# A chain of small transformer blocks on one core: transposes of the next tokens first, another vector order, values projected later, the feed-forward bias as a weight row

## The reference

```
x = x + attn_a(layernorm(x))         # latent attention, 16 heads
x = x + ffn4(layernorm(x))           # fp4-quantised gated feed-forward
x = x + forget_attention(layernorm(x))
x = x + ffn4(layernorm(x))
x = x + conv(layernorm(x))
x = x + local(layernorm(x))          # two layers, below
x = x + linear_attention(layernorm(x))
x = x + local(layernorm(x))          # the same two layers again
```

```
h = shift_token(x)                       # the second 64 columns come from the token before
q, k, v = split(h @ wqkv)                # 8 heads of 64
q, k = rotary(l2norm(q)*qs, l2norm(k)*ks)
x = x + softmax(q k^T in a window of 64, causal) v @ wo
h = layernorm(shift_token(x)) * lg + lb
a, g = split(h @ w1 + b1)                # 341 columns each
x = x + (a * gelu(g)) @ w2 + b2
```

## Time and profile before

| what | us |
|---|---|
| median of the runs shown | 2193.34 |
| the profiled execution's own time | 2203.51 |
| its span, first to last instruction | 2201.7 |
| PE busy | 1819.8 (83%) |
| DVE busy | 1407.5 (64%) |
| ACT busy | 942.4 (43%) |
| POOL busy | 454.2 (21%) |

### The profile page before, as it was taken

One profiled execution on the slowest core, in us unless ns is written; L12 is line 12 of the kernel. 1 busy time (PEld: TensorE's weight loads), 2 busy tenths in 40 slices (PEclk: granted clock), 3 DMA queues, 4 the chain that ended last, 5 costly groups with the idle time before them and its releaser, 6 DMA issues.

```text
span 2201.7 us, 34222 instructions
## 1 busy us (share of the span) xinstructions
PE 1819.8 (83%) x10946; PEld 1445.6 (66%) x11003; DVE 1407.5 (64%) x3623; ACT 942.4 (43%) x2559; POOL 454.2 (21%) x350
## 2 busy tenths in 40 slices
PE   7999966654566888898888799999968988888887
PEld 6888854222355777676676677777847766776676
DVE  4655689556896666676757445655547767566673
ACT  3444422110213555546454363353225464555544
POOL 2200010000013333332424100000014324233340
PEclk9999977555778999999999899999879999999998
DMA  3000000000100000000000000000000000000000
GB/s 133 0 0 0 1 0 0 1 0 0 48 0 1 3 1 2 3 2 4 1 2 1 3 1 0 0 0 0 0 1 4 2 2 1 4 2 3 2 1 22
DMA packets 15104, 13.89 MB, mean 6 GB/s; under 512 B 11286, under 2 KB 14138, under 8 KB 14650
## 3 DMA queue, kind: packets, MB, share of 16 engines
q1 hardware_dynamic: 15034, 13.01, 1.8%
HBM read 9.87 MB, written 1.05 MB: 5 GB/s over the span
## 4 chain that ended last, share of the span: by engine, by line
PE 45%; issue 30%; DVE 16%; ACT 7%; POOL 1%; DVEq 1%; POOLq 0%; ACTq 0%
PE bank L1558 5%; PE bank L1526 4%; PE bank L1546 4%; PE bank L1695 3%; PE bank L1642 3%; PE bank L1537 3%; DVE arena_attn L916 3%; PE bank L1655 2%; PE bank L1677 2%; DVE arena_ffn L901 2%; PE bank L1720 2%; PE bank L1699 2%; DVE probT L686 2%; ACT L1264 2%; PE bank L1743 2%
## 5 line engine op out<-in xcount | busy, mean ns | idle before, releaser
L534 POOL TENSOR_TENSOR arena_ffn<-arena_ffn 128x1024 f32<-128x1024 f32 x60 | 141.5, 2359 | 561.7 <-DVE arena_ffn L901 561.7
L686 DVE COPY probT<-bank 128x512 f32<-128x512 f32 x288 | 197.1, 684 | 70.7 <-PE bank L1537 70.4
L518 POOL TENSOR_TENSOR rstd<-var,mhalf 128x2 f32<-128x2 f32 x48 | 33.4, 696 | 902.6 <-DVE var L641 902.6
L1546 PE MATMUL bank<-vF,probT 128*128 128x64 f32 x1536 | 203.0, 276 | 1.7
L1546 PEld LDWEIGHTS bank<-vF,probT 128*128 128x128 f32 x1536 | 191.3, 196 | 12.9 <-DVE probT L686 12.2
L530 POOL TENSOR_TENSOR inv<-ssq,mhalf 128x16 f32<-128x16 f32 x64 | 188.2, 2940 | 33.6 <-DVE ssq L910 29.9
L1526 PE MATMUL bank<-arena_setup 128*128 128x192 f32 (+1 forms) x1024 | 171.6, 300 | 7.2 <-ACT arena_setup L1317 5.6
L679 DVE TENSOR_REDUCE nmaxF<-bank 128x2 f32<-128x384 f32 (+1 forms) x192 | 114.7, 597 | 88.9 <-PE bank L1526 88.9
L1368 ACT ACTIVATE arena_conv<-bank,nmaxF 128x192 f32<-128x192 f32 x256 | 105.6, 420 | 147.9 <-DVE nmaxF L679 95.1
L1526 PEld LDWEIGHTS bank<-arena_setup 128*128 128x128 f32 x1024 | 154.3, 191 | 11.8 <-issue 0.4
L897 DVE TENSOR_TENSOR arena_ffn<-bank,rope 128x512 f32<-128x512 f32 x128 | 87.7, 685 | 115.0 <-ACT arena_attn L1308 115.0
(11 more groups left out here) (258 smaller groups left out, 4302.4 us busy)
## 6 DMA issues: line engine op xcount, KB each, us to landing
packF<-in_packF SPq DMA_DIRECT2D x1, 3250.0 KB
arena_history<-in_packG SPq DMA_DIRECT2D x1, 2560.0 KB, 9.0
HS<-XH SPq DMA_DIRECT2D x32, 63.5 KB
X<-in_x_tiled SPq DMA_DIRECT2D x1, 1024.0 KB, 4.8
out_dram<-X SPq DMA_DIRECT2D x8, 128.0 KB, 1.9
arena_setup<-in_const_masks_a SPq DMA_DIRECT2D x1, 512.0 KB, 5.4
arena_setup<-in_const_masks_f SPq DMA_DIRECT2D x1, 512.0 KB
HS<-XH SPq DMA_DIRECT2D x32, 0.2 KB
```

The costliest lines, as they stand in the source:

```text
L534: pool.tensor_tensor(t1[:, t], t1[:, t], t2[:, t], ALU.add).then_inc(sems["rope_sum"], 1)
L686: dve.tensor_copy(probT[:, u % 2], bank[4 + u % 2][:]).then_inc(sems["pt_copied"], 1)
L1546: ins = pe.matmul(o, probT[:, u % 2, n * P:(n + 1) * P], val, start=first, stop=(kt == keys // P - 1), skip_group_check=True)
```

## The change

On PE the token transposes of the next batch come first in the step, behind a wait for the copies of v that was further down; the projections of both halves of v move to slot 8, behind the transposes of the output of half 0. On ACT the priming of the gelu table is taken out of `gelus`, and `shifted` comes between it and the gelus. On DVE `gated` moves ahead of the copy and rotary part of its slot, and `hidden_stats` behind the rotary part of slot 5. The bias b2 becomes row 341 of w2, that is row 113 of its third chunk; row 113 of the third chunk of ff is set to one by a fill on POOL once in each `local`, and `hidden_out` runs three matmuls of 114 rows for each half instead of four.

```diff
--- before.py
+++ after.py
@@ -69,7 +69,7 @@
 F_LAYOUT = []
 for _l in range(2):
     F_LAYOUT += [(f"wqkv{_l}", 3 * FH * FHD), (f"wo{_l}", 4 * C), (f"w1_{_l}", 2 * HID), (f"w2_{_l}", 3 * C),
-                 (f"ln_g{_l}", 1), (f"ln_b{_l}", 1), (f"b1_{_l}", 6), (f"b2_{_l}", C)]
+                 (f"ln_g{_l}", 1), (f"ln_b{_l}", 1), (f"b1_{_l}", 6)]
 G_LAYOUT = [("wqkvG", 3 * LH * LHD), ("wgG", LH * LHD), ("woG", 8 * C)]
 
 
@@ -372,7 +372,7 @@
         def zeros_by(n):
 
 
-            return N_POOL_FILL + sum((plan[m] == "conv") + (plan[m] == "win" and plan[m - 1] != "mlp")
+            return N_POOL_FILL + sum((plan[m] == "conv") + 2 * (plan[m] == "win" and plan[m - 1] != "mlp")
                             for m in range(n + 1))
 
         def opens(n):
@@ -592,6 +592,8 @@
                 if kind == "win":
 
                     pool.wait_ge(sems["xh_ready"], v.before("xh_ready"))
+                    pool.memset(ff[96:P, NCH - 1], 1.0).then_inc(setup_pool, 1)
+                    pool.wait_ge(setup_pool, zeros_by(n) - 1)
                     pool.memset(probW[:], 0.0).then_inc(setup_pool, 1)
                     if not opens(n - 1):
                         stage_copy(0)
@@ -947,12 +949,12 @@
                     if s < F_UNITS:
                         t, heads, keys = attn_unit(s, 2)
                         attn_max(v, i, s, len(heads), keys - F_FROM[t], nmaxF, F_SCORE_BANKS)
+                    if m and s == 1:
+                        gated(*m)
                     if s >= 2:
                         attn_copy(v, i, s - 2)
                     if m and s == 4:
                         mlp_end(m[0], m[1])
-                    if hid and s == 5:
-                        hidden_stats(*hid)
                     if nxt:
                         if s in (1, 4):
                             rope_part(vn, ni, nl, s // 4, 0)
@@ -962,8 +964,8 @@
                             norms(vn, ni, s // 6, sch)
                         if s == 7:
                             scaled(vn, ni, 0)
-                    if m and s == 1:
-                        gated(*m)
+                    if hid and s == 5:
+                        hidden_stats(*hid)
                     if hid and s == 7:
                         hidden_apply(*hid)
                     if s == 6:
@@ -1339,7 +1341,6 @@
 
             def gelus(v, i, l):
 
-                prime(ACT.Gelu)
                 for c in range(NCH):
                     n = FROWS[c]
                     src = (bank[7][0:n, 0:T], bank[7][0:n, T:2 * T], bank[6][0:n, T:2 * T])[c]
@@ -1355,10 +1356,12 @@
                 if nxt:
                     vn, ni, _ = nxt
                 if m:
+                    prime(ACT.Gelu)
+                if nxt:
+                    shifted(vn, ni)
+                if m:
                     gelus(*m)
                     prime(ACT.Exp, 1)
-                if nxt:
-                    shifted(vn, ni)
                 for u in range(F_UNITS):
                     t, heads, keys = attn_unit(u, 2)
                     act.wait_ge(sems["max_ready"], v.at("max_ready", i, u + 1))
@@ -1587,10 +1591,12 @@
                 v, nxt, m, hid = around(n, l, i)
                 if nxt:
                     vn, ni, nl = nxt
+                pe.wait_ge(sems["v_ready"], v.at("v_ready", i, NT))
+                if nxt:
+                    transpose_x(vn, ni, bank[2])
                 if m:
                     hidden_gates(*m, 0)
                 pe.wait_ge(sems["qkT_ready"], v.at("qkT_ready", i, NT))
-                pe.wait_ge(sems["v_ready"], v.at("v_ready", i, NT))
 
                 def scores(h, t, keys):
                     return qTF[:, h // 2, t * P:(t + 1) * P], keysZ[:, h // 2, h % 2, F_FROM[t]:keys]
@@ -1606,8 +1612,6 @@
 
                 def between(s):
 
-                    if nxt and s == 0:
-                        transpose_x(vn, ni, bank[2])
                     if m and s == 0:
                         pe.wait_ge(sems["down_used"], v.at("down_used", i, 0))
                         hidden_gates(*m, 1)
@@ -1615,10 +1619,11 @@
                         project_qk(vn, ni, nl, s // 4)
                     if m and s == 1:
                         hidden_values(*m)
-                    if nxt and s in (7, 8):
-                        project_values(vn, ni, nl, s - 7)
                     if s == 8:
                         transpose_y(0)
+                        if nxt:
+                            for t in range(NT):
+                                project_values(vn, ni, nl, t)
                     if m and s == 3:
                         hidden_out(*m)
                     if s == 3:
@@ -1671,11 +1676,9 @@
             def hidden_out(v, i, l):
                 pe.wait_ge(sems["f_ready"], v.at("f_ready", i, NCH))
                 for t in range(NT):
-                    pe.matmul(bank[7][:, t * P:(t + 1) * P], ones1[:], f_at[f"b2_{l}"][0:1, :], start=True, stop=False)
                     for c in range(NCH):
-                        n = FROWS[c]
-                        ins = pe.matmul(bank[7][:, t * P:(t + 1) * P], ff[0:n, c, t * P:(t + 1) * P],
-                                        f_at[f"w2_{l}"][0:n, c * C:(c + 1) * C], start=False, stop=(c == NCH - 1))
+                        ins = pe.matmul(bank[7][:, t * P:(t + 1) * P], ff[0:FCH, c, t * P:(t + 1) * P],
+                                        f_at[f"w2_{l}"][0:FCH, c * C:(c + 1) * C], start=(c == 0), stop=(c == NCH - 1))
                 ins.then_inc(sems["m_down_ready"], 1)
 
             def hidden_alone(v, i, l):
@@ -2032,8 +2035,8 @@
     for l in range(2):
         b1 = a["L1_ffn_b1"][l]
         f.update({f"wqkv{l}": a["L1_ffn_wqkv"][l], f"wo{l}": chunk_rows(a["L1_ffn_wo"][l], P), f"w1_{l}": a["L1_ffn_w1"][l],
-                  f"w2_{l}": chunk_rows(a["L1_ffn_w2"][l], FCH), f"ln_g{l}": a["L1_ffn_ln_g"][l][:, None],
-                  f"ln_b{l}": a["L1_ffn_ln_b"][l][:, None], f"b2_{l}": a["L1_ffn_b2"][l][None],
+                  f"w2_{l}": chunk_rows(np.concatenate([a["L1_ffn_w2"][l], a["L1_ffn_b2"][l][None]]), FCH), f"ln_g{l}": a["L1_ffn_ln_g"][l][:, None],
+                  f"ln_b{l}": a["L1_ffn_ln_b"][l][:, None],
                   f"b1_{l}": np.concatenate([chunk_rows(b1[:HID, None], FCH), chunk_rows(b1[HID:, None], FCH)], 1)})
     w["packF"] = pack(F_LAYOUT, f)
     w["packG"] = pack(G_LAYOUT, {"wqkvG": a["L1_attn_b_w_qkv"], "wgG": a["L1_attn_b_w_gate"], "woG": chunk_rows(a["L1_attn_b_w_out"], P)})
```

## The result

The changed kernel took 2237.51 us (median of 4 runs, 2236.01 to 2239.29), the kernel before beside it 2194.28 (4 runs, 2189.93 to 2195.74): ratio 1.0201, 95% interval 1.0183 to 1.0218. The forecast was 2184, range 2158 to 2206. The profiled execution took 2237.54; its span is 33.7 longer than before.

The account below looks back on a forecast made before the run. It took an ACT, PE, DVE chain in each step as the bound. Plain steps at -0.37 and the other steps and tails summed to -9.8 us: 2193.7 profiled, 2184 as median, range 2158 to 2206.

Parts of the forecast that it names:

- rival (c): PE waits ahead of the output transposes make the clock fall once a step, about +23 us, 2206; chance 0.14.
- finishing steps of the first `local`: Five steps that also finish a batch; forecast to come to 34.95 plus clock falls in three, -5.4 us together.
- tokens first: Next tokens' copies before the gelus on ACT: exponentials of unit 1 come 1.0 us earlier per plain step.
- bias row: Two bias matmul pairs leave PE's chain ahead of unit 1's transposes: 0.82 us a step, 1.15 with gate product first.
- gate product first: `gated` ahead of the rotary on DVE: the wait of 0.17 for it goes, 0.3 us from start to start.
- statistics behind the rotary: Hidden statistics later on DVE: POOL's sum starts later and clamp L910 ends 0.68 us later per plain step.
- values later, and the last ACT wait: Value projections between output transposes and unit 5's product, +1.6 us; ACT's wait for the last q and k closes, -0.5.
- the head: First part of a plain step: tokens first, bias row and gate product first bring unit 2's copy 2.15 us earlier.
- Rival (b): Clamp L910 issues ahead of POOL's sum, saving about 1.2 us in each of 28 steps: 2150; chance 0.15.
- (a): Wait for the last q and k stays, so plain and finishing steps gain nothing: 2193; chance 0.20.
- (d): Token copies find their transposes late, so the 1.0 us is lost in 26 steps: 2210; chance 0.06.
- The second steps: Second step of each `local`, with a hidden norm but no feed-forward: +1.8 us each, to near 30.2.

Follow-up runs that it names:

- experiment 14: Changed kernel with values and statistics as before, plus eight unused 128x128 PE transposes in slot 7: 2117.82 us, ratio 0.9616 to the kernel before.
- 13: Changed kernel with values and statistics as before, plus one unused 128x512 matmul in slot 7: 2117.74 us, ratio 0.9618 to the kernel before.
- 16: Changed kernel plus one unused 128x512 matmul ahead of each of PE's two waits (slots 7 and 8): 2179.93 us, ratio 0.9909 to the kernel before.
- kernel 2: Changed kernel with the values projected in their old place, slots 7 and 8: 2158.44 us, ratio 0.9827 to the kernel before.
- kernel 4: Kernel before with only the values moved to slot 8, behind the output transposes: 2267.75 us, ratio 1.0319 to the kernel before.
- 15: Kernel before with only the values moved, plus one unused 128x512 matmul ahead of each of PE's two waits: 2216.17 us, ratio 1.0067.
- 11: Changed kernel with values in their old place and hidden statistics ahead of the rotary as before: 2121.22 us, ratio 0.9665 to the kernel before.
- 10: Kernel before with only the next tokens transposed and copied first: 2165.17 us, ratio 0.9871 to the kernel before.
- 8: Kernel before with only the feed-forward bias as a weight row: 2167.29 us, ratio 0.9871 to the kernel before.
- kernel 3: Changed kernel with both values in slot 8 but ahead of the output transposes: 2145.3 us, ratio 0.9769 to the kernel before.
- experiment 9: Kernel before with only the values moved, plus both value projections made once more, unused, ahead of the wait for the attention output: 2263.49 us, ratio 1.0322.
- 5: Kernel 3 with POOL's rotary sum of half 1 ahead of the hidden deviation: 2173.9 us, ratio 0.9907 to the kernel before.
- 6: Changed kernel with POOL's rotary sum of half 1 ahead of the hidden deviation: 2230.47 us, ratio 1.0154 to the kernel before.
- kernel 7: Changed kernel with the hidden statistics ahead of the rotary part of slot 5 again: 2190.67 us, ratio 0.9994 to the kernel before.

## Why the prediction was wrong

**The step that failed is the dismissal of rival (c): the sum has nothing for a fall of the clock.** The prediction named the fall, and then said that by the rule on transposes "this rival becomes unlikely, 2184 stands; by idle time alone it is likely", and "the trace leans to the rule". It gave it 0.14. The rule in the Trainium skill (TensorE: Matmul & The Clock Gate, Part 4: PE-mode transpose), that transposes do not count as work for the clock gate, does not hold as it was used: eight transposes in a wait kept the granted clock at 1.00 in the plain steps of experiment 14, as a matmul did in 13. In the plain steps of the changed kernel the clock does not fall between the last value product and the output projection, where the prediction looked. It falls in PE's waits for the copied probabilities and for the output, and fillers in those waits stop it (16). These waits were forecast at 1.4 and 2.4 and are 1.45 and 2.16, or 1.30 for the second where the clock has already fallen and the product between them takes 1.97 in place of 1.10.

The prediction leaned on the finishing steps of the first `local`, and there its place is right: the clock falls at their end, behind waits of 1.28 and 0.72 among transposes. Before, the output projection (L1642) takes 2.84 at 1175.49 in place of 1.95, in kernel 13 it takes 3.21 at 1108.55, in spite of the filler further up. Where a plain step of kernel 2 has a fall, it comes in that stretch as well (granted clock 0.53 and 0.62 from 848 to 852), behind a wait of 1.25. No run filled those waits, so whether transposes count for less there stays open.

**Its size was off too.** The prediction priced a fall at 0.9 to 1.0, from steps before, where it hits the values of half 0 and the work behind them (granted clock 0.64 from 951 to 955 us) and costs 0.89. Here it hits the output transposes and both projections, which the change had just put in a row on the chain. From the start of the output transposes to those of q and k it is 4.71 in the short step shown, 5.81 in the long one and 3.05 in kernel 16: 1.66 and 2.76 more, and these are the differences of the whole steps (35.29 and 36.39 against 33.63). In the mean of the plain steps it is 35.86 - 33.63 = 2.2 each, in kernel 4 1.7. Over all stretches: 2237.51 against 2179.93, 58 us, or 1.8 a step of 32. Rival (c) reached 2206 and should have reached some 2240. It also counted one fall in five steps before, where 9 of the 26 plain and finishing steps have 0.95.

**The terms, at a clock of 1.00.** A cost of the fillers would be in the figures of 13, 15 and 16; 11, and the 1.69 of 15 above, show none.

| term of a plain step | predicted | measured |
|---|---|---|
| tokens first | -1.0 | -1.02 (10) |
| bias row | -1.15, with the gate product first | -1.03, alone (8) |
| both together | -2.15 | 34.62 to 32.03 = -2.59 (13) |
| statistics behind the rotary | +0.68 | 32.68 - 32.03 = +0.65 (2, 13) |
| values later, and the last ACT wait | +1.6 - 0.5 = +1.1 | 33.63 - 32.68 = +0.95 (16, 2); alone +1.26 (15) |
| sum | -0.37 | 33.63 - 34.62 = -0.99 |
| granted clock | 0 | +2.2 |

The schedule was thus read right and a little too darkly. The ACT wait stands with the values because it goes only with them: in kernel 13 the copies of v still start 5.84 ahead of the table load, in 16 5.11. The values term itself is what was forecast: from the output transposes to the product of unit 5 is 0.60 in kernel 2 (878.99 to 879.59) and 2.21 in 16 (881.97 to 884.18). What was sized too low is the head, by 0.4; the gate product first has no run of its own. Kernel 16 comes out where the forecast was (2180 against 2184), but only with work that computes nothing, and that the totals lie so close is partly luck: its profiled execution took 2179.3, 24 less than the one before, where the sum had 9.8.

**Rival (b)**, L910 not held, is refuted by the clamp at 928.66, which takes 1.27. **(a)** is refuted by the changed kernel's own trace, in which the wait for the last q and k is gone. **(d)** by the projection without a wait. The second steps, forecast at 30.2, took 33.08 and 32.18 at 0.90 and 0.89; kernel 16 has them at 30.3. The finishing steps of the first `local`, forecast at -5.4, moved by -0.8, and by -9.7 in kernel 16: the clock again.

**Statistics and values are not independent.** By medians the statistics cost 2158.44 - 2121.22 = 37 us with the values as before and 47 with them later, while the sum at 1.00 has 0.65 x 28 = 18. The profiles are the safer measure: the mean plain step differs by 32.77 - 32.38 = 0.39 with the values as before and by 35.86 - 34.98 = 0.88 with them later. A likely reason, not shown by itself, is that the later DVE gets to the output, the longer PE stands and the more the lowered clock takes.

What stays open: which amount of idleness brings the clock down. Kernel 2 waits 0.15, 0.17 and 1.25 in the plain step shown and holds 1.00 there and in 11 more; kernel 10 waits 1.20 ahead of the values of half 0 and falls in 15 of 16; kernel 3 waits 1.45 in each of two steps compared (843.68 and 876.37), and the clock falls in the second alone. No run separates them.

## What to carry over

Before moving PE work behind a wait, ask what PE does during that wait and what stands right behind it: an idle TensorE can come back at half its clock, and then the work just moved there is paid double. Price such a fall at the work on the chain behind the wait, not at the average of steps seen before, and test it with an unused matmul in each wait, including the first: a filler that stands only behind the first wait can be slowed itself, and then, as in experiment 9, it tells nothing. Do parts of a change one at a time: here two good parts of 1.3% each were hidden under two bad ones.

## What the hardware showed that was not expected

Small DVE instructions are held by POOL's addition of 128x1024: a clamp of 128x16 took 1.27 and one of 128x2 1.57, against 0.17 alone, and both ended with POOL's. That agrees with the Trainium skill (SBUF — State Buffer, Who interferes with whom), by which DVE and GpSimd share a pair of ports that the one to issue first can hold for its whole instruction, while the other is blocked. What the runs add is that moving POOL's addition only moves the victim (5 and 6).

The stretch between the two locals, which no experiment touched apart from its edges, took 411 to 435 us in the profiles, with the same busy time of DVE and ACT. Of kernel 3 and kernel 7:

```profile
1217.13:1628.65 411.52, 365.28 (x2310) 290.58 (x2311) 230.60 (x753) 168.48 (x318) 31.30 (x32) 0.94 0.00 0
```

```profile
1237.90:1672.58 434.68, 388.86 (x2310) 309.94 (x2311) 230.90 (x753) 168.30 (x318) 31.28 (x32) 0.89 0.00 0
```

The longer one is the one with the lower clock. It differs between executions of one kernel too: the profiled one of kernel 3, with the 411.52, took 2136.09, its median is 2145.3. Kernels 13 and 14 have the same mean plain step to 0.02; their profiled executions took 2117.57 and 2129.78, with 419 and 430 us in this stretch. So some 10 to 20 us between two profiles can come from a stretch that neither kernel changed, and step lengths at one granted clock are the safer measure.
